# The third batch's v is spread over its heads' rows by matmuls, as the last batch's is, and no longer through DRAM

## What is computed

```
r = (xr @ Wr.T).reshape(b, l, h, s_)
k = (xk @ Wk.T).reshape(b, l, h, s_)
v = (xv @ Wv.T).reshape(b, l, h, s_)
g = silu(xg @ Wg.T)
def step(s, rkvw):
    r_t, k_t, v_t, w_t = rkvw
    a = k_t[..., :, None] * v_t[..., None, :]
    out = einsum('bhi,bhij->bhj', r_t, u * a + s)
    s = a + w_t[..., :, None] * s
    return (s, out)
og = groupnorm(out) * gn_w + gn_b
x1 = x + og * g @ Wo.T
```

## Time and profile before

| what | us |
|---|---|
| median of 3 runs | 513.42 |
| the 3 runs | 508.31, 513.42, 544.58 |
| the profiled execution, whole | 513.0 |
| its span | 511.2 |
| what lies around the span | 1.8 |

### The profile page before, as it was taken

The page is one execution under the profiler, slowest core; times in us unless marked ns, Lnnn a source line. Parts: engine busy times, 40 slices in busy tenths (PEclk is TensorE's granted clock), DMA queues, the critical chain, the costliest instruction groups (busy, mean ns, idle before and its releaser), DMA issues.

```text
span 511.2 us, 7173 instructions
## 1 busy us (share of the span) xinstructions
PE 439.4 (86%) x2676; PEld 263.4 (52%) x2676; DVE 326.7 (64%) x623; ACT 215.3 (42%) x417; POOL 105.3 (21%) x103
## 2 busy tenths in 40 slices
PE   4988789899999999999899897999999896975465
PEld 2753323335774445577455355765462684662344
DVE  1245775733438578876897879688696646488342
ACT  1540523575636545643545455344558231400011
POOL 7350110010101004240100315220335101013000
PEclk9995955999999999999999999999999997996668
DMA  7799990350234274200237012001600000000001
GB/s 265 241 297 304 374 341 5 79 131 0 96 91 131 79 164 126 63 2 1 63 84 166 2 41 53 12 0 35 154 23 21 1 1 0 0 0 2 0 0 41
DMA packets 24137, 44.56 MB, mean 87 GB/s; under 512 B 2436, under 2 KB 18468, under 8 KB 22952
## 3 DMA queue, kind: packets, MB, share of 16 engines
q1 hardware_dynamic: 23112, 42.58, 28.3%
q10 hardware_dynamic: 992, 1.54, 0.9%
HBM read 29.53 MB, written 14.42 MB: 86 GB/s over the span
## 4 chain that ended last, share of the span: by engine, by line
PE 67%; DVE 21%; ACT 5%; issue 4%; DMA 1%; POOL 1%; SPq 0%; DVEq 0%; ACTq 0%; POOLq 0%
PE pW L432 10%; PE pO L490 8%; PE pMX L459 8%; DVE mx L979 8%; PE pST L473 7%; PE pW L515 6%; PE pW L577 5%; PE pW L586 5%; PE pW L528 4%; ACT probs L711 3%; DVE A L936 3%; PE pW L500 2%; PE pW L440 2%; PE pW L655 1%; DMA Wkq<-w_kq 1%
## 5 line engine op out<-in xcount | busy, mean ns | idle before, releaser
L979 DVE TENSOR_REDUCE mx<-pMX 128x1 f32<-128x512 f32 (+1 forms) x192 | 122.8, 685 | 46.2 <-PE pMX L459 44.8
L711 ACT ACTIVATE probs<-pST 128x512 f32<-128x512 f32 x192 | 104.2, 596 | 63.4 <-PE pST L473 62.0
L459 PE MATMUL pMX<-Kst,Qst 97*128 97x512 bf16 (+1 forms) x256 | 72.1, 358 | 14.3 <-DVE mx L979 13.8
L473 PE MATMUL pST<-Qst,Kst 99*128 99x256 bf16 x384 | 65.2, 282 | 1.8 <-ACT probs L711 0.2
L490 PE MATMUL pO<-probs,Vn 128*32 128x256 f32 x768 | 63.5, 403 | 0.3 <-ACT probs L711 0.3
L473 PEld LDWEIGHTS pST<-Qst,Kst 99*128 99x128 bf16 x384 | 30.3, 99 | 42.1 <-ACT probs L711 23.6
L459 PEld LDWEIGHTS pMX<-Kst,Qst 97*128 97x128 bf16 x256 | 20.7, 100 | 58.7 <-DVE mx L979 45.1
L936 DVE TENSOR_TENSOR_SCAN A<-four,COL,A 128x256 f32<-128x256 f32 x64 | 48.9, 825 | 0.3
L515 PE MATMUL pW<-hT,Wkq 128*128 128x256 f32 (+1 forms) x96 | 34.1, 507 | 7.3 <-DMA Wkq<-w_kq 7.3
L1111 DVE SCALAR_TENSOR_TENSOR A<-pW,COL,A 128x256 f32<-128x256 f32 (+1 forms) x24 | 13.0, 570 | 27.3 <-ACT A L757 18.5
L843 POOL TENSOR_TENSOR A<-A 128x1024 bf16<-128x1024 f32 x8 | 17.0, 2128 | 60.7 <-ACT A L725 60.7
(11 more groups left out here) (139 smaller groups left out, 601.2 us busy)
## 6 DMA issues: line engine op xcount, KB each, us to landing
Kst<-k_stack SPq DMA_DIRECT2D x16, 576.0 KB
A<-v_rows SPq DMA_DIRECT2D x6, 1024.0 KB, 9.6
k_stack<-A SPq DMA_DIRECT2D x8, 576.0 KB, 4.3
k_stack<-A SPq DMA_DIRECT2D x8, 384.0 KB, 2.9
Qst<-q_stack SPq DMA_DIRECT2D x16, 192.0 KB
hT<-hT SPq DMA_DIRECT2D x3, 768.0 KB, 4.8
q_stack<-A SPq DMA_DIRECT2D x16, 128.0 KB, 3.3
Wsq<-w_sq SPq DMA_DIRECT2D x1, 2048.0 KB, 14.4
```

The costliest lines, as they stand in the source:

```text
L459: last = mm(pMX[n % 2][:, at:at + hi - lo], Qst[s][0:R_MASK + 1, h, qt * P:(qt + 1) * P], Kst[s][0:R_MASK + 1, h, lo:hi], start=True, stop ...
L473: last = mm(pST[n % ST_BANKS][:, i, :], Kst[s][0:R_LO + 1, h, nt * P:(nt + 1) * P], Qst[s][0:R_LO + 1, h, :], start=True, stop=True)
L711: act_fn(probs[n % UNITS_P][:], pST[n % ST_BANKS][:], ACT.Exp, scale=1.0 / DH)\
L979: v.tensor_reduce(dst, src, AX.X, ALU.max).then_inc(max_done, 1)
```

## The change

Batch 2 moves from `TAIL` to `TAIL_V`: `PE_V` becomes (2, 3), and the order string gets the two streams' runs fitted to the new list of steps. The write and the two spread reads through DRAM, and the steps kv0 and kv1 of batch 2, are gone; eight units vk00 to vk13 and their eight products are there. The matrix `spread` is now made at batch 2's step x. Since `TAIL_V` has another order than `TAIL`, `ruk`, `g` and `rs00`, `rs10`, `rs01` of batch 2 also change their places.

```
-PE_V = (3,)
+PE_V = (2, 3)
...
-         "12 22 1 m x2 s x 2 m 25 m2 22 1 m3 x m x m 23 m x2 m2 x m x2 m4 22 x 12 x3 2 m 24 12 x3 2 3 23 x13 2 x9 22 "
...
+         "12 22 1 m x2 s x 2 m 25 m2 22 1 m3 x m x m 23 m x2 m2 x m x2 m4 24 x 12 x3 m 23 12 x3 3 28 x22 25 33 23 33 "
```

## The result

| | before | after |
|---|---|---|
| median, us | 510.87 (4 runs) | 524.02 (4 runs: 522.84 to 526.42) |
| ratio | 1 | 1.0282, 95% interval 1.0236 to 1.0328 |
| span of the profiled execution | 511.2 | 521.6 |

The change makes the kernel slower by 2.8%; the forecast was 526.7 on 513.0, which is 2.7%. Taken by itself, 526.7 lies above all four runs. The ratio leaves out the one run of before at 544.58, which fell into a slower state of the chip, so it is not the quotient of the two medians.

A forecast was written before the change was run, and what follows sets the result against it. TensorE was taken as the bound until the attention ends at about 395.3. From 513.0, + 8.1 (exp 14 2 late) - 0.3 (stages) + 4.4 (tail) + 1.5 (clock) = 526.7 us; range 520.5 to 531.

The forecast's parts named there:

- DRAM way and kv1, kv0: gain: Batch 2's removed DMAs, kv1 on GpSimd and kv0 on VectorE: 0 gained, at best the GpSimd wait of 0.50 us.
- eight units less g 2, in the attention's end: TensorE ahead of exp 14 2: eight vk units add 6.9 us, g 2 leaving takes away 1.8.
- first wait: Ahead of rr 1: xr 1 is queued behind vk01's product on VectorE, so TensorE idles 1.4 us.
- second wait: Ahead of vk13: it needs vk10's bank, whose product stands behind scan01 on VectorE; TensorE idles 1.7 us.
- exp 14 2 late by: Start of the last ten attention stages, late by 8.1 us from units and both waits; ends 5.1 and 9.1.
- last ten stages: Attention's exp 14 2 to pv 15 5: -0.3 us since g 2's tanh is gone; ends 0 and -0.6.
- oq 7 to up0, clock aside: Tail after the attention: g 2, then diag waiting for ruk behind scan11, add 4.4 us; ends 1.8 and 5.1.
- clock: Behind TensorE's idle of 2.8 us ahead of diag: diag, oT and proj partly at lower clock, 1.5 us.
- up0 to the end: Stretch behind up0, same order in both kernels: stays 105 us; any other value would show the prediction wrong.
- rival of the hidden units: Last ten stages: ScalarE's exponentials bind and hide TensorE's new units, total 517.1 us; chance 0.10.
- rival 1: Tail behind the gap ahead of diag: the clock stays up, without the 1.5, total 525.2 us; chance 0.27.
- VectorE against GpSimd: x 3 on GpSimd starts about 387.9, when scan01 is about to end: 0 us; other end 1.0.

The follow-up runs named there:

- ninth: Kernel before with g 2 placed behind proj 3 and the step gate of batch 2 behind rms 3 and z 3; ratio 1.0038.
- sixth: Kernel before with unit g 2 placed behind proj 3; ratio 1.0088.
- second experiment: Changed kernel with vk13 of batch 2 behind pv 14 1 instead of ahead of exp 14 2; r 2 to up0 49.0 us, from 49.3.
- fifth experiment: Kernel before with scan11, ruk and g of batch 2 placed ahead of diag, the changed kernel's tail order; ratio 1.0105.
- tenth kernel: Changed kernel with all placements of the fourth, and gate of batch 2 behind z 3; ratio 1.0197.
- first: Changed kernel with xr 1 placed ahead of vk00 of batch 2; r 2 to up0 46.5 us, from 49.3.
- seventh: Changed kernel with every matmul of batch 2's eight vk units issued twice; ratio to the kernel before 1.0332.
- eleventh experiment: Changed kernel profiled a second time, nothing changed; span 522.5 us, up0 to the end 104.7.
- third experiment: Changed kernel with scan11 and ruk of batch 2 placed ahead of oq 7; median 520.7 us, ratio to the kernel before 1.0227.
- fourth: Changed kernel with the placements of first, second experiment and third experiment together, and g 2 behind proj 3; ratio to the kernel before 1.0225.

## Why the prediction was right

| step of the prediction | forecast | measured |
|---|---|---|
| DRAM way and kv1, kv0: gain | 0 | 0 in the kernel before (0.35 and 0.58 in the ninth and sixth) |
| eight units less g 2, in the attention's end | 6.9 - 1.8 | 5.5 more when doubled (6.9 less the filled wait of 1.16 is 5.7) |
| first wait | 1.4 | 1.13 (1.4 gained without it) |
| second wait | 1.7 | 1.16 (1.3 gained without it) |
| exp 14 2 late by | 8.1 | 8.0 |
| last ten stages | -0.3 | 7.8 - 8.0 = -0.2 |
| oq 7 to up0, clock aside | 4.4 | 14.9 - 10.6 = 4.3 |
| clock | 1.5 | 1.4 |
| up0 late by | 13.7 | 13.4 |
| up0 to the end | 105 | 102.1, then 104.7 |

**What bounds.** TensorE was the bound of the last stages, as the earlier trace rows say. The doubled matmuls show it best; the second experiment shows that a unit between the stages fares no better. The rival of the hidden units falls.

**The waits.** Both were there with the releasers that were named, 0.3 and 0.5 shorter than forecast. In part VectorE got through its queue sooner, since a row's busy time overlaps the next (scan01, in a row with 2.67, is followed by the product 2.58 later). In part it is the way of counting: the working ends exp 13 5 after 0.44, but its row has 0.60 with the drain, and the profile counts the gap from there. The starts are nearer than the gaps: rr 1 is late by 3.0, where 3.1 was forecast.

**The tail.** g 2's 1.8 and the wait for ruk behind scan11 made 4.3, and the fifth experiment has the same 4.3 (14.9 against 10.6) in a kernel without the change's units. With the order repaired, the tenth kernel is still 42.2 - 35.9 = 6.3 behind the ninth at up0, which has the same tail and the way through DRAM. That is the price of the eight units, 6.9, less the ninth's own wait for xr 1, 0.4, within 0.2. The other 7 of the 13.4, about half, are the order that came with the list TAIL_V and the clock behind its gap, not the spread by matmuls: the tail's 4.3 less the 1.5 to 1.8 that g 2 left free in the stages, the two waits and the clock's 1.4.

**The DRAM way.** Its price was put at 0, with GpSimd's 0.5 as the best. That was nearly so in the profiled execution of before, but for a reason that I had not seen: kv1 holds xr 1 on VectorE, 1.16 instead of 0.88 in the earlier trace rows, 2.04 in the sixth experiment, where it cost TensorE 0.58. How much depends on when the DMA lands. The prediction's list missed this term; it is small.

**The clock.** I gave a fall the better chance and its size fits. One row was read too short: that vk13 ran at the full level behind the gap of 2.02 did not clear that gap, since the very next unit had the 3.36 shown above. The same gap of 2.44 was followed by slow units in both profiles of the changed kernel and in the second experiment, and by none in the first, fifth and seventh. So rival 1 was as near the truth as the forecast, and the runs tell only that it can go both ways. That the 1.5 came true in the changed kernel's own profiles is in part luck.

**The number.** The profiled execution took 523.4, 3.3 less than 526.7: 0.3 from the terms up to up0, 0.4 ahead of r 2, and 2.6 behind up0, where the prediction had the stretch fixed at 105 and named any other value as a sign of being wrong. That sign appeared in the first profile. The eleventh experiment shows that it was not the program; the step that was too simple is that equal order means equal time. Both sides of the ratio carry such differences, and that 2.7% and 2.8% agree so closely is luck.

**VectorE against GpSimd.** x 3 started at 387.82, as forecast (387.9), and scan01 was done at 387.45, so the term of 0 held. The next scan, scan10, was the one that x 3 and rs00 held, for 5.51 instead of 2.67, and nobody waited for it.

**What stays open.** The tenth kernel's four runs lie between 514.9 and 522.56; the one that was profiled is the shortest. What the others lost, and where, was not seen. 6.3 us at up0 would be a ratio of 1.012, which the tenth's interval still holds. Open is also what sets whether a gap is followed by the lower clock, and why the executions reach r 2 up to 6 us apart.

## What to carry to other kernels

Work that leaves a transfer for the engine that binds is paid in full, even where the transfer looked expensive: ask first whether anyone waited for it. When a variant of a step list is reused at another place, compare the whole list, not the steps that give it its name: here scan11 and ruk, standing behind oq 7, cost 4 of 13 us (the third experiment). And when a producer is moved back, look at each queue in which its consumers stand ahead of something urgent, GpSimd's with its tiny but critical rms above all.

## What the runs showed of the hardware

Some VectorE operations that ran beside a GpSimd operation were held until about its end: z 1.62 instead of 0.62, xr 2.04 instead of 0.88, and in the changed kernel scan10 5.51 instead of 2.67, beside four GpSimd operations in a row; the last was hidden. Others were not held. The products of vk, which read PSUM and one SBUF operand, kept their 0.63 to 0.69 in all profiles, and a reduction that reads one tensor from SBUF (L1055, at 481.58 in the kernel before) kept 0.69 beside a multiplication of 1.27. For z this goes further than I had reckoned with: it reads one tensor from SBUF, not two. The Trainium skill names both cases in SBUF — State Buffer, "Who interferes with whom": `tensor_scalar` can use a mode that needs the shared pair of ports, and then contends. The 1.62 agrees, but no run here shows the mode itself.

The granted clock behind a gap of 2.44 us was full in three executions and at the lower of its two levels in three others, with the same ten stages, oq 7 and g 2 ahead of it. Behind the gap of 2.02 the next unit was slow in five profiles of fourteen; behind gaps of 2.75 (late in batch 3's tail, in all fourteen) and of 4.04 (in the fourth and sixth) it was slow or partly slow each time. So a gap of 2.0 to 2.4 us has a chance of a price and not a price: 1.4 to 2.3 us here from oq 7 to up0 (16.25 and 17.24 against 14.9), and nothing where TensorE waits again anyway, as behind g 3.
